# Keys stored in four copies instead of six, three value chunks moved into the unit loop, and a reordered start

## What is computed

```python
x = x + _L0_xattn_ref(_layernorm(x), ctx_1024, mask, wq, wk, wv, wo)      # 16 heads of 8 dims, 2048 keys
x = x + _L0_attn_ref(_layernorm(x), ...)                                  # causal latent attention
x = x + _L0_ffn_ref(_layernorm(x), ...)                                   # one of 8 matrices, chosen by argmax
x = x + _L1_xattn_ref(_layernorm(x), ctx_1024, ctx_1024, ...)             # 16 heads of 8 dims, 2048 keys
x = x + _L1_attn_ref(_layernorm(x), ...)
x = x + _L1_ffn_ref(_layernorm(x), ...)                                   # router and experts
```

```python
logits = einsum('btnh,bfnh->bnft', k, q * 8 ** -0.5) + bias
weights = softmax(logits, axis=-1)
attn = einsum('bnft,btnh->bfnh', weights, v)
```

## Time and profile before

| | us |
|---|---|
| median of 3 runs | 303.58 (301.65 to 303.95) |
| the profiled execution | 304.16 |
| its span in the trace | 301.9 |
| PE busy | 278.7 (92%) |
| DVE busy | 222.3 (74%) |
| ACT busy | 207.0 (69%) |
| POOL busy | 72.0 (24%) |

### The profile page before, as it was taken

How to read it: one execution, slowest core, us unless ns; L and a number is a source line. 1 busy time by engine, 2 the same in 40 slices (tenths; PEclk the granted TensorE clock), 3 DMA queues, 4 the chain that set the end, 5 groups by cost and what they waited for, 6 DMA issues and landing times.

```text
span 301.9 us, 10317 instructions
## 1 busy us (share of the span) xinstructions
PE 278.7 (92%) x4414; PEld 179.2 (59%) x4418; DVE 222.3 (74%) x372; ACT 207.0 (69%) x427; POOL 72.0 (24%) x143
## 2 busy tenths in 40 slices
PE   6978799979989999889999999889999999899995
PEld 5444467647666655454555666557766665436675
DVE  5875389959989984555377999889899960744583
ACT  7863288959998988813445689879989997133350
POOL 5601356411011121421022676001011030110001
PEclk9998799979999999999999999999999999999999
DMA  7993503943222291282300018623223200000000
GB/s 244 410 400 90 178 26 123 346 179 88 86 72 87 72 285 55 103 319 89 123 1 2 1 56 284 255 92 87 76 65 97 58 2 2 2 0 2 0 0 24
DMA packets 12692, 33.82 MB, mean 112 GB/s; under 512 B 1077, under 2 KB 2197, under 8 KB 12262
## 3 DMA queue, kind: packets, MB, share of 16 engines
q1 hardware_dynamic: 12596, 33.11, 32.0%
q10 hardware_dynamic: 50, 0.03, 0.0%
HBM read 20.42 MB, written 12.71 MB: 110 GB/s over the span
## 4 chain that ended last, share of the span: by engine, by line
PE 57%; DVE 14%; DMA 12%; issue 6%; ACT 6%; POOL 2%; SPq 2%; ACTq 0%; DVEq 0%; POOLq 0%
PE bank L1201 55%; DMA kpair<-k_scratch 10%; DVE mx L926 9%; DMA k_scratch<-kparts 3%; ACT probs L616 2%; SPq L303 1%; DVE s_neg L1010 1%; POOL kparts L435 1%; DVE o_rec L875 1%; DVE k_rest L883 1%; SPq L329 1%; PE bank L1581 0%; DVE xn L847 0%; DVE kparts L887 0%; ACT L737 0%
## 5 line engine op out<-in xcount | busy, mean ns | idle before, releaser
L926 DVE TENSOR_REDUCE mx<-bank 128x2 f32<-128x1024 f32 x128 | 151.6, 1216 | 21.5 <-PE bank L1201 20.4
L616 ACT ACTIVATE probs<-bank 128x512 f32<-128x512 f32 x256 | 140.0, 596 | 17.4 <-PE bank L1201 13.5
L1201 PE MATMUL bank<-probs,v_all 128*9 128x128 f32 x2048 | 80.8, 276 | 2.2 <-ACT probs L616 1.5
L1201 PE MATMUL bank<-q_exp,kpair 64*128 64x128 bf16 x1024 | 81.5, 218 | 1.1 <-ACT q_exp L539 1.1
L1201 PE MATMUL bank<-kpair,q_rows 64*128 64x512 bf16 x256 | 70.8, 388 | 9.3 <-DMA kpair<-k_scratch 7.3
L1201 PEld LDWEIGHTS bank<-q_exp,kpair 64*128 64x128 bf16 x1024 | 54.9, 94 | 28.3 <-ACT probs L616 17.1
L1201 PEld LDWEIGHTS bank<-probs,v_all 128*9 128x9 f32 x2048 | 43.6, 90 | 19.1 <-ACT probs L616 4.6
L477 POOL CAST m_rows<-negm 128x2 bf16<-128x2 f32 x32 | 6.2, 193 | 116.2 <-DVE negm L933 116.2
L1201 PEld LDWEIGHTS bank<-kpair,q_rows 64*128 64x128 bf16 x256 | 21.5, 93 | 16.3 <-DMA kpair<-k_scratch 8.8
L539 ACT ACTIVATE v_all<-bank 128x512 f32<-128x512 f32 (+1 forms) x20 | 10.6, 539 | 17.5 <-PE bank L1201 17.4
L394 POOL TENSOR_TENSOR y<-ve,mhalf 128x1 f32<-128x1 f32 (+1 forms) x10 | 5.8, 580 | 53.7 <-DVE ve L834 53.7
(11 more groups left out here) (237 smaller groups left out, 348.0 us busy)
## 6 DMA issues: line engine op xcount, KB each, us to landing
kpair<-k_scratch SPq DMA_DIRECT2D x62, 192.0 KB
k_scratch<-kparts SPq DMA_DIRECT2D x8, 768.0 KB, 4.7
k_scratch<-kparts SPq DMA_DIRECT2D x8, 512.0 KB, 6.0
ctxT_s<-in_ctxT SPq DMA_DIRECT2D x4, 512.0 KB, 8.2
mask_s<-in_mask SPq DMA_DIRECT2D x2, 1024.0 KB, 8.9
k_scratch<-kparts SPq DMA_DIRECT2D x8, 256.0 KB, 7.5
wM<-in_packM SPq DMA_DIRECT2D x1, 1728.0 KB, 9.5
wB<-in_packB SPq DMA_DIRECT2D x1, 654.0 KB, 8.9
```

The costliest lines, as they stand in the source:

```text
L616: act.activation(probs[:, j % 4, :], slot_bank(l, "b", n, j), ACT.Exp).then_inc(S("slot_free"), 1)
L926: V.tensor_reduce(mx[n % 2][:, w, :], bank[:, 2 * (w % 2):2 * (w % 2) + 2, :], AX.X, ALU.max) \
L1201: return T.matmul(out_, lhsT=lhsT, rhs=rhs, start=start, stop=stop, **kw)
```

## The change

Four things change. (1) The scratch holds four copies of the keys, not six: high once, middle twice, low once. Each head's load becomes two DMAs of 24 rows: one reads the eight high rows three times (a source dimension of size 3 with step 0), the other the three remaining copies. A pair's load is then four DMAs of 96 KB, and `K_LOADS` counts them. (2) Value chunks 5, 6 and 7 of layer 0, used from unit 8 on, leave the start and are made in units 3, 5 and 6, in a ring slot each. (3) The sum for the flag stands ahead of value chunk 3, and the first `early_k` ahead of the branch. The other three follow the first three score products, so that GpSimd splits one key chunk ahead of unit 0 (`K_LATE` 3). In layer 1 the last `early_k` moves behind the second score product. (4) `put_exp(0)` of layer 0 stands ahead of the sixth score product.

```diff
-K_LOADS = 2
+K_LOADS = 4
-V_BANK = ((2, 3, 6, 7, 4, 5, 4, 5), (7, 3, 7, 6, 4, 5, 4, 5))
+V_BANK = ((2, 3, 6, 7, 4), (7, 3, 7, 6, 4, 5, 4, 5))
-K_LATE = (4, 4)
+K_LATE = (3, 4)
+V_UNIT = {3: 5, 5: 6, 6: 7}
...
-        kscr = nc.dram_tensor("k_scratch", (2, B, len(SLOTS), H, HD, SK), BF16, kind="Internal").ap()
+        kscr = nc.dram_tensor("k_scratch", (2, B, 4, H, HD, SK), BF16, kind="Internal").ap()
...
-            src = kscr[l, b, :, p * 2 + a, :, :]
-            eng.dma_start(kpair[u][a * HOFF:a * HOFF + HR, :], src).then_inc(S(f"k_loaded{u}"), 16)
+            row = a * HOFF
+            high = kscr[l, b, 0, p * 2 + a, :, :].unsqueeze(0).to_broadcast([3, HD, SK])
+            eng.dma_start(kpair[u][row:row + K_BASE[1], :], high).then_inc(S(f"k_loaded{u}"), 16)
+            rest = kscr[l, b, 1:4, p * 2 + a, :, :]
+            eng.dma_start(kpair[u][row + K_BASE[1]:row + HR, :], rest).then_inc(S(f"k_loaded{u}"), 16)
...
-                    first = K_BASE[kp] // HD
+                    first, times = (0, 1, 3)[kp], (1, 2, 1)[kp]
...
-                    sp.dma_start(dst, src.to_broadcast([P, K_TIMES[kp], SK // 2])).then_inc(S(f"k_stored{b}"), 16)
+                    sp.dma_start(dst, src.to_broadcast([P, times, SK // 2])).then_inc(S(f"k_stored{b}"), 16)
...
+                def values_late(n):
+
+                    slot_ready(0, "v", n)
+                    for i in range(4):
+                        last = v_tile(slot_bank(0, "v", n)[:, i * P:(i + 1) * P], 0, 4 * V_UNIT[n] + i)
+                    last.then_inc(S("slot_full"), 1)
...
-                    if l == 0 and i == 0:
-                        pe.wait_ge(S("v_copied"), 4)
-                        early_k(0, 0)
-                    elif l == 0 and i == 1:
+                    if l == 0 and i < 3:
+                        early_k(0, i + 1)
+                    elif l == 0 and i == 3:
                         pe.wait_ge(S("q_rows2"), 2)
                         prep_v(0, 4)
-                    elif l == 0 and i == 2:
-                        early_k(0, 1)
-                    elif l == 0 and i == 3:
-                        prep_v(0, 5)
-                        early_k(0, 2)
                     elif l == 0 and i == 4:
-                        prep_v(0, 6)
-                        early_k(0, 3)
-                    elif l == 0 and i == 5:
-                        prep_v(0, 7)
...
+                        put_exp(0)
...
+                        if k == 1 and n in V_UNIT and l == 0:
+                            values_late(n)
```

More of the change, by code:

```diff
@@ L83 @@
 FOLDS = (0, 1, 2)
+V_UNIT = {3: 5, 5: 6, 6: 7}
+V_FIRST = (0, 5)
 RING_BANK = (4, 5, 6)
@@ L325, in store_k @@
                 for kp in range(PARTS):
-                    first = K_BASE[kp] // HD
-                    dst = kscr[l, b, first:first + K_TIMES[kp], :, :, t:t + SK // 2].rearrange("s h d t -> (h d) s t")
+                    first, times = (0, 1, 3)[kp], (1, 2, 1)[kp]
+                    dst = kscr[l, b, first:first + times, :, :, t:t + SK // 2].rearrange("s h d t -> (h d) s t")
                     src = kparts[:, kp, b * SK + t:b * SK + t + SK // 2].unsqueeze(1)
-                    sp.dma_start(dst, src.to_broadcast([P, K_TIMES[kp], SK // 2])).then_inc(S(f"k_stored{b}"), 16)
+                    sp.dma_start(dst, src.to_broadcast([P, times, SK // 2])).then_inc(S(f"k_stored{b}"), 16)
             def load_k(l, p, b, u):
@@ L653, in take_fold, with take_v @@
                     last.then_inc(S("slot_free"), 1)
+                def take_v(n):
+                    act.wait_ge(S("slot_full"), slot_no(0, "v", n))
+                    copy_v(0, V_UNIT[n], slot_bank(0, "v", n)).then_inc(S("slot_free"), 1)
                 k1_after = {(14, 6): 0, (15, 0): 1, (15, 2): 2, (15, 4): 3}
@@ L658, in cross @@
                         stage_k(0, i)
-                        prep_v(0, 4 + i)
+                    prep_v(0, 4)
                 else:
@@ L675, in cross @@
                             take_fold(n)
+                        if j == 3 and n in V_UNIT and l == 0:
+                            take_v(n)
                         if j == 3 and n in PIECES and l == 1:
@@ L1224, in early_k @@
                     pe.wait_ge(S(f"in_ctx{2 + i // 2}"), 16)
-                    if i >= 2:
-                        pe.wait_ge(S("k_staged"), i - 1)
+                    if i < 3:
+                        pe.wait_ge(S("v_copied"), i + 2)
+                    else:
+                        pe.wait_ge(S("k_staged"), 2)
                 elif i >= 2:
@@ L1236, in prep_v @@
                 if used:
-                    pe.wait_ge(S("v_copied"), 8 * l + used[-1] + 1)
+                    pe.wait_ge(S("v_copied"), V_FIRST[l] + used[-1] + 1)
                 for i in range(4):
@@ L1398, in b_unit @@
                         pe.wait_ge(S("slot_free"), slot_no(l, "q", n))
-                    if n == 0 and j < 2:
-                        pe.wait_ge(S("v_copied"), 8 * (l + 1))
+                    if l and n == 0 and j < 2:
+                        pe.wait_ge(S("v_copied"), V_FIRST[1] + 8)
                     slot_ready(l, "b", n, j)
@@ L1449, in cross @@
                 for i, (n, w) in enumerate([(0, 0), (0, 1), (0, 2), (0, 3), (1, 0), (1, 1)]):
-                    if l and i == 1:
-                        pe.wait_ge(S("k_staged"), 7)
+                    if i == 1:
+                        pe.wait_ge(S("k_staged"), 7 if l else 1)
                     a_ready(n, w)
@@ L1455, in cross @@
                     if l and i == 1:
+                        early_k(1, 3)
                         half_query(1, 6, P)
@@ L1667, in _ @@
             prep_v(0, 2)
-            prep_v(0, 3)
             pe.wait_ge(S("flag_rows"), 1)
@@ L1673, in _ @@
             mm(bank[0:1, 2, 0:1], flag_f[:, 2:3], ones_col, start=False).then_inc(S("flag_sum"), 1)
+            prep_v(0, 3)
+            early_k(0, 0)
             def from_cross(masked):
@@ L1680, in from_cross @@
                 early_k(1, 0)
-                pe.wait_ge(S("v_copied"), 8 + 2)
+                pe.wait_ge(S("v_copied"), V_FIRST[1] + 2)
                 early_k(1, 1)
```

27 lines of the change are left out of this document (13 added, 14 removed).

## The result

| | before | after |
|---|---|---|
| median, us | 303.76 (301.65 to 305.83, 4 runs) | 326.21 (324.09 to 331.83, 4 runs) |
| after : before | | 1.072, interval 1.061 to 1.082 |
| the profiled execution | 304.16 | 326.89 |
| its span | 301.9 | 324.8 |
| mean granted TensorE clock | 0.983 | 0.968 |

The kernel became 7.2% slower: 326 us, where 329 were forecast, in a range of 308 to 345. The ratio leaves out the execution of 331.83 us, whose mean clock (0.948) was lower than that of the other three. From the page of after: the shares of the chain that ended last, PE's group of key products, and the DMA issues of the pair loads.

What follows compares the result with a forecast made beforehand. Bounds: PE's own work and a loop of key load and use. To 304.16 us it added 3.5 (pair 8), 6.3 and 10.8 (units), 1.2 (value chunks), 1.5 (stores), 2 (clock), less 0.3: 25.0 in all, so 329, range 308 to 345.

Steps and rivals of the forecast that it cites:

- Three engines: Pair loads: each of three copies runs on three engines, not six; DMA share 0.20, near 78 GB/s.
- Rival A: Pair loads do not get slower, so the change gains what its bytes promise: 298 us; chance 0.11.
- Landing 8.7 us behind issue: Pair loads: issue to landing grows by 2.5 us, from 6.2 to 8.7.
- 0.9 us a unit: Loop of load and use: a unit takes 6.05 us, 0.9 more than 5.14; 6.3 us over pairs 9 to 15.
- Rival C: Loop has more slack than read, a unit staying at 5.04 or 5.14 us: 310 us; chance 0.10.
- The start: Up to pair 8: first load at 21.7, gain of 1.5 us at pair 3, pair 8 used 3.5 us late.
- The end of layer 0: 11.0 us late: 3.5 at pair 8, 6.3 for pairs 9 to 15, 1.2 for value chunks.
- Layer 1: Pairs 16 to 19 covered; pairs 20 to 31 lose 10.8 us, stores 1.5, the start gains 0.3.
- Layer 1's key chunk: Start of layer 1: moving it frees two score products 1 us earlier, gaining 0.3 us, 1.0 at most.
- The clock: PE's half clock behind longer gaps ahead of pairs 3, 5 and 6: 2 us lost in all.
- Rival B: Clock falls in nearly every unit, 0.75 us a unit more, 14 us over 19 units: 341 us; chance 0.13.
- Waits in nearly every unit: PE's waits for key loads rise from 7.3 us to some 25 to 35, in nearly every unit.

Runs made afterwards that it cites:

- three copies alone: The kernel before, with each head's load cut into two DMAs of three copies, stores and order unchanged: 331.35 us, 1.087 of before.
- the order edits alone: The kernel after with the storage and loads of before (six copies, two loads a pair), so only the moved work remains: 306.03 us, 1.003 of before.
- row-outermost kernel: The kernel after with each load's 24 rows in another order, key row first and copy second, outermost dimension 8: 295.21 us, 0.971 of before.
- with the chunk back: The row-outermost kernel with layer 1's last key chunk put back ahead of the first score product: 294.17 us, 0.968 of before.

## Why the prediction was right, point by point

**Three engines** held: share 0.18 to 0.20, 73 to 81 GB/s, in both kernels with loads of three copies and in both layers. By the rule of the Trainium skill (DMA: Bandwidth & Descriptors, section "Why a DMA increments its semaphore by 16 and not by 1") it would be 3, 6, 8 and 16 engines for the four layouts run here; their shares of 0.20, 0.40, 0.49 and 1.02 agree.

**Four DMAs a pair cost nothing** held: four with six copies are at 0.997 of before. **Rival A**, loads that don't get slower, falls by the same runs; the kernel with rows in another order comes nearest to what it would have given, at 295.2, though on eight engines and not six, where 298 was worked out.

**Landing 8.7 us behind issue** was too much: 7.8 for pairs 12 and 26, 8.3 for pair 31. Issue to first use, by which the loop goes, averages 8.5 us over pairs 9 to 15 and 8.0 over pairs 24 to 31, so layer 0 came near the forecast and layer 1 did not. What was mis-sized is the 6.2 us it started from, or the growth of 2.5, or both. The 6.2 was issue to use of pair 8, named an upper bound and then used as the value. The growth can be read where both kernels wait: with three copies alone, pair 1's issue to use went from 6.95 to 9.11 us and pair 15's from 7.86 to 9.91, so by 2.1 to 2.2. Taken from 7.8 that leaves 5.3 to 5.7 us for a quiet load of before, an estimate, since no wait shows one. The pause that was allowed for each added DMA isn't there.

**0.9 us a unit** was about right in layer 0: uses of pairs 8 to 15 are (121.95 - 77.97) / 7 = 6.28 us apart, and before (110.57 - 73.65) / 7 = 5.27, so 1.0 more, of which pair 15's late landing has a share. In layer 1 it was too much. Issues of pairs 24 to 31 are (254.84 - 215.02) / 7 = 5.69 us apart, for 5.24 before: 0.45 more (by their first uses 0.56). That is about what a landing of 7.8 leaves in the sum of the prediction: two units take 7.8 + 3.4 = 11.2, 5.6 each. Rival C, more slack than read, was a part of the truth here: the period lies between its 5.14 and the forecast's 6.05.

**The start** held in its times: first load issued at 21.90 (21.7), exponent rows at 30.41 (31.5), pairs 1, 2, 3 at 30.09, 36.65, 43.15 (31.1, 36.6, 43.6), pair 8 at 77.97 (77.1). PE's wait for pair 1 was 3.63 us, and the 5 us promised by the order edits shrank to 1.9 at pair 3. Three engines are not shown to be the reason: pair 3 did wait 1.01 us for its load, but the order edits alone, on six engines and without such a wait, reached it only 1.8 us early as well, at half clock for 10.24 us. Pair 8's time came out in part by luck. Its load was issued at 66.42, 2 us sooner than worked out, and its use at 77.97 shows no wait for it: what made it late is pair 7's wait of 2.49 us and the half clock from 72.49 on.

**The end of layer 0** came 11.4 us late (11.0). Three value chunks were counted at 1.2 us together; at full clock and without load waits they cost 2.8 (three times 0.9). In the kernel after a part of that lies under the waits for loads, so neither figure can be read from its total.

**Layer 1** gave 22.8 - 11.4 = 11.4 us from pair 15 to pair 31, where 10.8 + 1.5 - 0.3 = 12.0 stood. Its terms were off against each other. Its quiet units were 0.45 and not 0.9; against that, 1.7 us was lost up to pair 17 (13.1 late, pair 15 11.4), where loads were counted as covered, and 6.83 us at half clock in 209.02:215.85 stood in the sum only as a part of 2 us for all. **Layer 1's key chunk** had the wrong sign: 0.3 us of gain was counted, and it is worth nothing or costs 0.2. The use of pair 17 follows pair 16's by 5.53 us in place of 4.67, and most of that had been gained ahead of pair 16: its use follows pair 15's by 51.18 us in the row-outermost kernel, by 51.80 with the chunk back.

**The clock** was counted at 2 us. From the mean clock of a span comes its time at half speed: before (1 - 0.983) x 301.9 x 2 = 10.3 us, after (1 - 0.968) x 324.8 x 2 = 20.8 us, for there it is 0.50. Before, it comes in pieces like the 3.41 us of the earlier trace rows; after, in four stretches of 6.83, 3.41, 3.41 and 6.83, 20.5 in all. Where PE was the bound, 6.83 us cost 2.6; ten more would cost 3.9 by that, and less where a load is waited for. That the sum came so near is in part luck: a landing counted too late and a clock counted too kindly have opposite signs. **Rival B**, half clock in nearly every unit, falls: four stretches, not nineteen.

**Waits in nearly every unit** was too strong, and 25 to 35 us a little high: 19 waits, 23.3 us. Of the 22.9 us that the span grew, 16.0 are more waiting for loads. The other 6.9 would be met by ten more us at half clock (up to 3.9) and the value chunks (up to 2.8); that split is my estimate from the two prices above, and no run took both away alone.

## What to carry to other kernels

Before a load is cut or its copies are shared, look at the outermost dimension of the source of every new DMA: 3 x 8 rows and 8 x 3 rows are the same bytes and here 31 us apart. A small total of waits does not say that loads have slack; compare issue to landing with issue to use, in a stretch where a wait ends one: this kernel showed 7.3 us of waits and had 10 us to win by wider loads, and 22 to lose by narrower ones. Work that is taken from in front of a wait has to go somewhere, and should be costed at full rate there, as the wait it leaves behind may cost the clock too.

## What the runs showed of the hardware that was not expected

A load's issue on SP was shorter for the load that goes to all 16 engines, and didn't grow from three engines to eight. That load is also one run of 48 rows, where the others have an outermost dimension of their own, so which of the two shortens the issue is not shown. Issues of the pair loads in three kernels (least, median and most ns of one, then first and last), of three copies, eight rows outermost, and 48 rows in one run:

```profile
L305 SPq DMA_DIRECT2D kpair<-k_scratch x124: 677/678/1035, 24.6 to 264.0; - x124
```

```profile
L308 SPq DMA_DIRECT2D kpair<-k_scratch x62: 651/653/869, 21.9 to 222.8; - x62
```

```profile
L303 SPq DMA_DIRECT2D kpair<-k_scratch x62: 302/422/1148, 24.8 to 222.8; - x62
```

The median is 678, 653 and 422 ns. Between 16 and eight engines the time of the kernel did not differ (293.2 and 292.5); PE waits 0 and 0.3 us for key loads in them.

The other is the clock at the start: the same instructions up to layer 1 got the full clock in one execution and 0.50 for 6.83 us in another. The row-outermost kernel's own six times stand in two groups, 292.14 and 292.16, and 294.87 to 295.85; the distance, 2.7 to 3.7 us, is about the 2.6 us that 6.83 us at half clock cost at that place. The mean clock on record is 1.000 for the first group and 0.983 to 0.988 for the second, so the groups do differ by the clock. That it falls at the start in all of the second is not shown, since only the execution of 292.16 was profiled. What decides it stays open.
